# A decoder's cross attentions: three small steps on a head's maxima move from VectorE to GpSimd

## The reference, cut to what matters

```python
q = split_heads(x @ Wq + bq); k = split_heads(ctx @ Wk + bk); v = split_heads(ctx @ Wv + bv)
scores = einsum('bhqd,bhkd->bhqk', q, k) / sqrt(16)
scores = where(mask == 0, -1e9, scores)        # first layer only
attn = softmax(scores, axis=-1)
out = einsum('bhqk,bhkd->bhqd', attn, v) @ Wo + bo
x = layernorm(x + out)
```

## Time and profile before

| | us |
|---|---|
| median of three runs | 2865.86 (2857.93 to 2866.38) |
| the profiled execution, its own time | 2858.85 |
| its span in the trace | 2857.1 |
| TensorE busy | 2657.4 (93%) |
| VectorE busy | 2143.4 (75%) |
| ScalarE busy | 1802.5 (63%) |
| GpSimd busy | 533.8 (19%) |

### The profile page before, as it was taken

The page is one execution under the profiler, slowest core; times in us unless marked ns, Lnnn a source line. Parts: engine busy times, 40 slices in busy tenths (PEclk is TensorE's granted clock), DMA queues, the critical chain, the costliest instruction groups (busy, mean ns, idle before and its releaser), DMA issues. The chain is left out here.

```text
span 2857.1 us, 93546 instructions
## 1 busy us (share of the span) xinstructions
PE 2657.4 (93%) x39187; PEld 1001.4 (35%) x39187; DVE 2143.4 (75%) x5870; ACT 1802.5 (63%) x2158; POOL 533.8 (19%) x742
## 2 busy tenths in 40 slices
PE   4999999999999999948999998999999999999997
PEld 1623333432222222324222224662222222266664
DVE  7689999479999999485899994139999999551115
ACT  2288888627777777733888886233888888822222
POOL 0078782030000000002222113212000000003330
PEclk8899999979999999978999999997999999999999
DMA  3456652241111110202111112010122221121112
GB/s 101 123 116 158 140 130 75 71 150 26 28 28 27 27 29 18 74 13 88 40 43 43 44 47 89 0 65 26 46 64 56 56 57 35 39 95 39 44 44 89
DMA packets 122804, 177.27 MB, mean 62 GB/s; under 512 B 38835, under 2 KB 89918, under 8 KB 122128
## 3 DMA queue, kind: packets, MB, share of 16 engines
q1 hardware_dynamic: 103344, 124.55, 16.5%
q0 software_dynamic: 13568, 46.17, 5.9%
q10 hardware_dynamic: 5472, 0.56, 0.2%
HBM read 131.75 MB, written 31.96 MB: 57 GB/s over the span
## 5 line engine op out<-in xcount | busy, mean ns | idle before, releaser
L811 DVE TENSOR_REDUCE mpart<-ps 128x1 f32<-128x512 f32 x1536 | 978.9, 683 | 77.2 <-PE ps L598 73.8
L598 PE MATMUL ps<-stack 48*32 48x512 f16 (+4 forms) x13312 | 939.5, 349 | 41.6 <-DVE mpart L811 12.8
L523 ACT ACTIVATE xT<-ps,exp_scale 128x1024 f32<-128x1024 f32 (+3 forms) x800 | 785.1, 1028 | 215.6 <-PE ps L619 107.0
L523 ACT ACTIVATE cn<-ps,exp_scale 128x1024 f32<-128x1024 f32 (+4 forms) x800 | 733.2, 959 | 155.2 <-PE ps L619 73.8
L619 PE MATMUL ps<-stack 50*32 50x512 f16 (+3 forms) x11648 | 761.3, 371 | 32.2 <-ACT xT L523 24.3
L598 PEld LDWEIGHTS ps<-stack 48*32 48x32 f16 x13312 | 276.5, 90 | 986.4 <-DVE mpart L811 515.1
L804 DVE CUSTOM_DVE_ANT_0 scrap<-ps,arena 128x512 bf16<-128x512 f32 x768 | 490.1, 686 | 40.7 <-PE ps L598 37.3
L668 PE MATMUL ps<-xT,vall 128*17 128x512 f32 (+4 forms) x3648 | 412.5, 512 | 2.6 <-POOL xT L482 1.7
L668 PE MATMUL ps<-cn,vall 128*17 128x512 f32 (+3 forms) x3392 | 408.4, 501 | 1.2 <-ACT cn L523 1.0
L619 PEld LDWEIGHTS ps<-stack 50*32 50x32 f16 x11648 | 202.2, 90 | 190.9 <-ACT xT L523 96.0
L788 DVE CUSTOM_DVE_ANT_0 scrap<-ps,scrap 128x128 bf16<-128x128 f32 (+3 forms) x512 | 247.3, 484 | 14.3 <-PE ps L598 8.9
(11 more groups left out here) (293 smaller groups left out, 2778.9 us busy)
## 6 DMA issues: line engine op xcount, KB each, us to landing
stack<-q_parts SPq DMA_DIRECT2D x384, 64.0 KB, 3.2
stack<-k_parts SPq DMA_DIRECT2D x192, 64.0 KB, 3.3
wbuf<-in_maskT POOLq DMA_DIRECT2D x48, 256.0 KB, 4.7
arena<-in_moe_w SPq DMA_DIRECT2D x19, 512.0 KB, 4.8
stack<-k_parts SPq DMA_DIRECT2D x192, 50.0 KB, 2.4
stack<-sums_inverse SPq DMA_DIRECT2D x16, 512.0 KB, 6.0
parts<-osb SPq DMA_DIRECT2D x240, 32.0 KB
wbuf<-in_mask POOLq DMA_DIRECT2D x16, 401.0 KB, 4.3
```

What stands on the lines that cost most here:

```text
L523: nc.scalar.activation(e.prob[tile % P_SLOTS][0:rows, half * HALF + first:(half + 1) * HALF], S_PS(g)[0:rows, first:HALF], ACT.Exp, scale= ...
L598: last = nc.tensor.matmul(bank[quarter(j), i * w:i * w + w], qs[b][rows, at:at + 32], ks[b][rows, a:a + w], start=True, stop=True)
L811: nc.vector.tensor_reduce(dst, src, AX, ALU.max).then_inc(unit_used, 1)
```

## The change

In the two cross attentions (`causal` false) the steps between the reduce and the turn go to GpSimd. There are now six steps: VectorE does step 0 (the reduce) and step 5 (the turn), GpSimd does four, because the fused multiply and add becomes a multiply into a new buffer `mback` and an addition. All six still form one chain through `max_chain`. On VectorE the turn stands where it stood, before unit 4 of the next head, with no step before units 1, 2 and 3. GpSimd's steps for head 0 stand behind the wait for the bias row and ahead of the additions and the shifts; those for heads 1 to 15 stand behind them. The self-attentions keep five steps on VectorE. `scale_ahead` and `invert(0)` stay behind unit 5.

```diff
-        MAX_STEPS = 5
+        MAX_STEPS = 5 if causal else 6
+        own_steps = {u: u for u in range(5)} if causal else {0: 0, 4: 5}
...
                 pool.wait_ge(ahead_in, 16 * len(ahead))
 
+                def part_maxima(h):
+
+                    high, low = (e.mneg[:, i * NT:(i + 1) * NT] for i in range(2))
+                    pool.wait_ge(max_chain, MAX_STEPS * h + 1)
+                    nc.gpsimd.tensor_scalar(e.mrest, e.mfin, -1.0 / MAX_UNITS[1], None, ALU.mult).then_inc(max_chain, 1)
+                    pool.wait_ge(max_chain, MAX_STEPS * h + 2)
+                    nc.gpsimd.tensor_scalar(high, e.mrest, MAX_UNITS[1] / MAX_UNITS[0], None, ALU.mult).then_inc(max_chain, 1)
+                    pool.wait_ge(max_chain, MAX_STEPS * h + 3)
+                    nc.gpsimd.tensor_scalar(e.mback, high, -MAX_UNITS[0] / MAX_UNITS[1], None, ALU.mult).then_inc(max_chain, 1)
+                    pool.wait_ge(max_chain, MAX_STEPS * h + 4)
+                    nc.gpsimd.tensor_tensor(low, e.mback, e.mrest, ALU.add).then_inc(max_chain, 1)
+
+                if not causal:
+                    part_maxima(0)
+
                 def add_bias(t):
...
                     for t in range(NT):
                         add_bias(t)
+                if not causal:
+                    for h in range(1, H):
+                        part_maxima(h)
                 if masks_ahead:
...
-                    if step == 1:
+                    if step == MAX_STEPS - 1:
+                        if h:
+                            dve.wait_ge(max_out, 16 * h)
+                        made = nc.vector.transpose(e.mturn, e.mneg)
+                    elif step == 1:
                         made = nc.vector.tensor_scalar(e.mrest, e.mfin, -1.0 / MAX_UNITS[1], None, ALU.mult)
...
-                    elif step == 4:
-                        if h:
-                            dve.wait_ge(max_out, 16 * h)
-                        made = nc.vector.transpose(e.mturn, e.mneg)
...
-                        if u < MAX_STEPS:
-                            finish_max(h - 1, u)
+                        if u in own_steps:
+                            finish_max(h - 1, own_steps[u])
                         unit(h, u)
...
-                for step in range(MAX_STEPS):
+                for step in own_steps.values():
                     finish_max(H - 1, step)
...
+        e.mback = sb("mback", NT)
```

More of the change, by code:

```diff
@@ L920, in _ @@
                     for u in range(nu):
-                        if u < MAX_STEPS:
-                            finish_max(h - 1, u)
+                        if u in own_steps:
+                            finish_max(h - 1, own_steps[u])
                         unit(h, u)
-                        if h == 1 and u == MAX_STEPS and reach_of is not None:
+                        if h == 1 and u == 5 and reach_of is not None:
                             scale_ahead()
-                        if h == 12 and u == MAX_STEPS:
+                        if h == 12 and u == 5:
                             nc.vector.memset(sums[1], 1.0).then_inc(parts_set, 1)
                             invert(0)
-                for step in range(MAX_STEPS):
+                for step in own_steps.values():
                     finish_max(H - 1, step)
```

## The result

| | us |
|---|---|
| changed kernel, median of 6 runs | 2872.07 (2870.58 to 2874.71) |
| kernel before, median of 6 runs | 2858.64 (2856.52 to 2866.38) |
| ratio | 1.0045, 95% interval 1.0035 to 1.0056 |
| profiled execution of the changed kernel; its span | 2872.47; 2870.7 |

The change costs 12.9 us by the ratio (10.0 to 16.0); the two spans differ by +13.6. The forecast was +18.8 us, slower, and 2881 us as the new time (2866 to 2893).

A forecast was written before the change was run, and what follows sets the result against it. TensorE was taken to set the first cross attention's pace, TensorE and VectorE together the second's. Start +21.0, steady state -2.7 and last heads +0.5 gave +18.8 us: 2877.7 or 2884.7 by base, middle 2881, range 2866 to 2893.

The forecast's parts named there:

- the start of the first cross attention: Head 0's GpSimd steps delay additions, residual write, mask loads and first maxima in turn: +21 us, ends +16.5 and +23.
- the last heads: After a cross attention's last head no units cover GpSimd's chain, so the turn comes later: +0.5 us, ends 0 and 1.3.
- the small DMA behind the masks: First maxima's DMA on SyncE's queue waits behind 2 MB of masks: +21; rival that it passes them: +17, chance 0.25.
- The shifts' price of nothing: First cross attention: GpSimd's shifts end at 645.6, before any product, costing nothing while SyncE is later than that.
- The clock adds nothing: First cross attention's start: clock already granted at 0.50 (1.2 GHz), rising only after the scores have begun, now as then.
- The gain in steady state: VectorE loses three steps a head, 0.24 us: -0.7 us in the first cross attention, -2.0 in the second, together -2.7.
- GpSimd's chain: Four GpSimd steps of 0.27 us plus five hand-overs of 0.03: 1.2 us, within 2.35 us between reduce and turn.
- The rival of slow steps: GpSimd steps of 0.9 us each make VectorE wait 1.4 us at 30 turns: 15 to 42 us more, chance 0.10.
- VectorE's relief pays more than its own time: Rival, not slower: freeing VectorE removes nearly all TensorE idling in both cross attentions, -24 us, deciding at -12; chance 0.04.
- The signs named beforehand: Wrong if second cross attention's head period shortens by over 0.24 us, or first's scores come within 10 us of the reduce.

The follow-up runs named there:

- the second experiment: The changed kernel with the first maxima sent right after the residual's write, ahead of the four mask loads, in the first cross attention: 2866.86 us, ratio 1.0036.
- the third experiment: The changed kernel with the first maxima sent by SyncE ahead of its wait for the additions: 2859.29 us, ratio 1.0003.

## Why the prediction was right, and where it missed

The direction and the cause were forecast, and +18.8 us came out as +13.6 between the two spans. Of the 5.2 us, 3.5 are a gain that was sized too small, 1.0 the start of the first cross attention, 0.5 the last heads and 0.2 the rest. As a time, 2881 us stood a further 3.6 us too high, because it started midway between a single run of 2858.85 and a median of three at 2865.86, where six runs have 2858.64. The range's ends don't follow from their own terms either: 2858.85 + 17 - 5.3 is 2870.6 and 2865.86 + 23 + 1.3 is 2890.2, where the text has 2866 and 2893. The measured 2872.07 lies inside both.

**The first cross attention's start: right, step by step.** Every step of the working stands in the trace. The trace's times are in brackets: chain over at 626.2 (626.24), additions over at 637.2 (637.15), SyncE's write at 637.4 (637.18), first maxima at 646.3 (645.32), second half at 652.6 (650.84), scores at 654.8 (652.78). The scores moved by 19.3 us instead of 21. Two sizes were off: the residual's write landed in 6.32 us, not 7.15, and the small DMA behind the masks in 5.52 instead of 6.3. That it stands behind them, a choice the rows before left open, is shown by the second experiment. The shifts' price of nothing held, with the condition that the text gave; the third experiment puts 7.9 us on it when the condition goes.

**"The clock adds nothing" was not quite right.** Of the +19.99 us between the reduces of head 0 and 1, the scores' move accounts for 19.44 (28.18 against 8.74 us from reduce to scores). The other 0.55 us comes after the scores. Slices of TensorE's clock and the first product, in the kernel before, then in the changed one:

```profile
637.00:639.00 2.00, 2.00 (x40) 0.58 (x28) 1.93 (x6) 1.31 (x2) 0.00 (x0) 0.50 0.73 99
639.00:641.00 2.00, 2.00 (x44) 0.48 (x36) 0.65 (x3) 1.04 (x2) 0.00 (x0) 0.92 0.00 0
...
638.65 1.37 PE L668 MATMUL ps<-xT,vall 128*17 128x512 f32 x8
```
```profile
658.00:660.00 2.00, 2.00 (x20) 0.16 (x20) 0.14 (x2) 1.02 (x1) 0.00 (x0) 0.50 0.56 96
660.00:662.00 2.00, 2.00 (x56) 0.59 (x40) 1.77 (x5) 1.29 (x2) 0.00 (x0) 0.99 0.00 0
...
657.74 1.91 PE L687 MATMUL ps<-xT,vall 128*17 128x512 f32 x8
```

The clock rose from 1.2 to 2.4 GHz about 5.8 us after the first scores where TensorE had been busy with units, and about 7.2 us after them where it had been idle for 19 us. The first product, 5.0 to 5.1 us behind the first scores, ran across the rise in the one kernel, in 1.37 us, and wholly at 1.2 GHz in the other, in 1.91. These 0.54 us are the size of what is missing. No experiment changed the clock alone.

**The gain in steady state: mechanism right, size wrong, and this is the step that missed most.** The working took 0.7 + 2.0 us, and its upper ends were 1.7 and 3.6. Measured are 2.84 and 3.35. In the second cross attention the steps' own 3 x 0.08 us a head were given back whole, where the working discounted them to 2.0 because the waits were "partly at other places"; the waits of the earlier trace rows fell by 3.7 us. In the first, the failing sentence is the one that capped the first cross attention's gain at "the 1.7 us of idle time": TensorE gave back 2.84 us where the rows showed 1.72 us of idle. The two timelines of TensorE show where it was. The kernel before, units (L598) and scores (L619) after the reduce at 698.59:

```profile
700.13 0.40 PE L598 MATMUL ps<-stack 48*32 48x512 f16 x4
...
700.84 0.40 PE L598 MATMUL ps<-stack 48*32 48x512 f16 x4
700.85 0.60 PE L619 MATMUL ps<-stack 50*32 50x512 f16 x8
701.54 0.40 PE L598 MATMUL ps<-stack 48*32 48x512 f16 x4
...
703.06 0.40 PE L598 MATMUL ps<-stack 48*32 48x512 f16 x4
```

And the changed kernel, the same after the reduce at 718.21:

```profile
719.76 0.40 PE L617 MATMUL ps<-stack 48*32 48x512 f16 x4
...
720.42 0.39 PE L617 MATMUL ps<-stack 48*32 48x512 f16 x4
720.44 0.59 PE L638 MATMUL ps<-stack 50*32 50x512 f16 x8
720.96 0.40 PE L617 MATMUL ps<-stack 48*32 48x512 f16 x4
...
722.49 0.40 PE L617 MATMUL ps<-stack 48*32 48x512 f16 x4
```

From the first start to the last it is 2.93 us before and 2.73 after, and no start has an idle time in brackets. From the second unit shown to the third it is 0.70 us, then 0.54. Only 0.09 us of the 0.70 is free of recorded matmuls (701.45 to 701.54); the rest of the stall lies inside recorded durations. Over the 14 heads the stretch of the earlier trace rows got 2.70 us shorter (its ends are set 0.14 us off the reduces' 2.84): recorded idle time fell by 1.16 us (1.72 to 0.56), and busy time by 1.54 (502.48 to 500.94) for the same 10820 matmuls. So more than half of what was won had been recorded as work. The experiments bear the price out, 0.07 to 0.08 us for each step and head where the steps stand; only the single step put back on VectorE cost less in the usual head of the first cross attention, 0.04 us.

**GpSimd's chain: right, a little short.** The forecast's 1.2 us run from the end of the reduce. Counted so, the chain took 1.42 us for head 0 (624.82 to 626.24) and 1.32 for the head at 718.21. Each constant scaling took 0.25 us (0.27 taken, 0.15 to 0.52 bounded), but from start to start of dependent ones it is 0.34 us, so a hand-over costs 0.09 us and not 0.03. That 626.24 is so near to 626.2 is luck: the reduce came 0.17 us earlier in this trace. The chain fits the room of 2.35 us, as forecast. The rival of slow steps had 15 to 42 us for 42 us of lateness, and the chain made slow cost 0.7 to 1.0 us for each us.

**The last heads: cost nothing** (0.5 taken, 0 its lower end). The turn was 0.7 us later, and the DMA behind it still landed before the scores needed it: the scores stand 6.04 us after the reduce in both kernels. The first of the two DMAs took 2.82 us in the trace before, from which the forecast was made, and 1.98 in the changed one.

**The rival that won nothing.** "VectorE's relief pays more than its own time" was right in its direction: the relief paid twice the forecast, though no more than the steps' own 0.24 us a head. It would have needed 12 us.

**The signs named beforehand.** None came that would have made it wrong, but one stood at its mark: a head's period in the second cross attention got shorter by 0.24 us (3.35 us in 14 heads), where more than 0.24 was the sign. The first scores of the first cross attention came 28 us after the reduce, those of the second 10.5 us after it against 10.7.

The sum with the measured terms: +20.0 - 2.84 - 3.35 - 0.2 = +13.6 us.

## What to carry to other kernels

A wait put at the head of an in-order queue delays all that stands behind it, and then what waits for those on other queues: four small steps on GpSimd, 1.3 us in all, placed ahead of 29 unrelated instructions, turned a gain of 6 us into a loss of 13. Follow the queue through every engine before you price the moved work itself, and put such a wait behind whatever is ready earlier. An engine's idle time in a trace is no upper bound for what it can give back, since work can be recorded as busy while it waits (1.54 of 2.70 us here); compare the distances between starts of the same instructions instead. And a small instruction has no price of its own: it costs its issue time where the engine is behind, and little or nothing where it waits for others.

## What the runs showed of the hardware

- A DMA of 8 KB issued behind 2 MB on the same queue landed in 5.52 us, ahead of them in 1.98.
- GpSimd scales 128x16 by a constant in 0.25 us and adds 128x16 in 0.22; dependent ones start 0.34 us apart.
- TensorE's granted clock rose from 1.2 to 2.4 GHz some 7.2 us after the first scores where TensorE had idled 19 us before them, and some 5.8 us after them where it had been busy at 1.2 GHz.
- In the masked cross attention a turn that came 0.97 us late cost 0.69 us in a usual head; in the other, 1.05 us late cost 1.04.
